# A two-layer transformer tower on one core: the next image's layer norm in nine pieces inside the local attention's loop, its transposes in front of the output product

## The chip, the cores and the metric

The kernel runs on one core of one Trainium2 chip. Its engines are named as in the profile: PE (TensorE, with PEld for its weight loads), DVE (VectorE), ACT (ScalarE), POOL (GpSimd) and SP (SyncE, which issues DMAs here). SBUF is the on-chip memory of 128 partitions, PSUM the eight banks that PE writes into. The metric is the time of one execution on the device in microseconds (us); lower is better. Durations of single instructions are given in us as well, unless marked ns.

## The reference, cut to what matters

Four images are turned into 1024 tokens of 64 numbers each. A first block adds local attention (16 query heads, one shared key and value head, every token looks at itself and the 128 before it) and a mixture of eight experts; a second block adds full attention with a batch norm, and another mixture. The change touches the first norm and the local attention:

```
h = tokens(x)                                  # 4 images x 1024 tokens x 64
n = (h - mean(h)) / sqrt(var(h) + 1e-5)        # layer norm over the 64
q, k, v = n @ wq.T, n @ wk.T, n @ wv.T         # q: 16 heads, k and v: one head
q, k = rmsnorm(rope(q)), rmsnorm(rope(k))
s = where(0 <= row - col <= 128, q @ k.T / 8, -1e30)
h = h + concat_heads(softmax(s) @ v) @ wo.T
h = h + experts(layernorm(h)); ...
```

The norm of an image needs nothing but that image's tokens. All of it is float32.

## The kernel before

The program is a row of stages with a barrier of all engines between them: `setup`, `tokens`, then for each of the four images `project` and `windowed` (a loop of the hardware over `b`), then the later layers. The tokens of an image are made one image ahead: `project` for image b also makes the tokens `h_next` of image b + 1 (a part of the tile `hl`), and `windowed` for image b also norms them and turns them, so that `project` for image b + 1 finds them in `xT`. The work on the next image in the last of the four rounds is done too, and not used.

`windowed` goes over 32 chunks of 32 tokens, as a pipeline that every engine runs in its own program order. In iteration n:

- PE makes the scores of chunk n (`scores`: two mask products L620, four products L624), turns the probabilities of chunk n - 3 (`turn`, ten transposes L637) and makes the values of chunk n - 4 (`values`, L654 and L651). `scores(n)` waits until ACT is done with the exponentials of chunk n - 2, whose two PSUM banks it writes.
- DVE takes the row maxima of chunk n (L684), turns them into the bias of the exponential (L687), copies the turned probabilities of chunk n - 3 from PSUM (L695), and inverts the sums of chunk n - 1 (L701), which waits for ACT's exponentials of that chunk.
- ACT makes the four exponentials of chunk n (L736, each with a read of its accumulated sum), and between them copies an earlier chunk's values to `oT` (`outputs`, L724).
- POOL scales the probabilities of a chunk as soon as DVE has inverted its sums (L715 and L717, both from SBUF to SBUF).

After the loop PE makes the output product of the attention (L669, 16 products of 512 columns) once ACT has copied the last chunk (`oT_ready`), then the four transposes of the normed tokens (`turn_normed`, L273), then the four transposes of the attention's output (`turn_halves`, L396), which wait for ACT's copy of it (L743, `v_act`). DVE norms the next tokens after its last copy of the loop (`layernorm`, L220 to L227, with `one_over_root`, L235 to L240, a Newton iteration on eight columns), copies half of the turned tokens (`turned_vector`, L285; ACT copies the other half, `turned_scalar`, L280) and adds the attention's output to the tokens (L705), which is the stage's last operation.

Every step of `layernorm` but the last goes through `ch.step`: it counts a semaphore up and DVE waits for that count before it goes on. The norm's result goes to `xn` (a part of `vwin`), its scratch is `vrem` and `pTr_own`, which the loop uses as well.

Of the kernel before, what the change touches and what calls it, by code (L numbers as in the profile page):

```python
# [19 lines left out]
I32 = mybir.dt.int32  # L20
U32 = mybir.dt.uint32
ALU = mybir.AluOpType
# [5 lines left out]
D = 64  # L28
# [50 lines left out]
def program(nc, inp, out, sent_rows, answered_rows):  # L79
    with ExitStack() as ctx:  # L80
# [147 lines left out]
                            bc(stat[:, 4, :tiles], D).rearrange("p (w j) d -> p w j d", w=2),  # L228
                            ALU.mult).then_inc(S["xn_ready"], 1)

        def one_over_root(v, ch, dst, x):

            n = x.shape[1]
            half, y, t = (newton[:, k, 0:n] for k in range(3))
            ch.step(v.tensor_scalar(half.bitcast(I32), x.bitcast(I32), 1, None, ALU.logical_shift_right))  # L235
            ch.step(v.tensor_scalar(y.bitcast(I32), half.bitcast(I32), -1.0, float(0x5F3759DF), ALU.mult, ALU.add))
            for k in range(3):
                ch.step(v.tensor_tensor(t, y, y, ALU.mult))
                ch.step(v.scalar_tensor_tensor(out=t, in0=t, scalar=-0.5, in1=x, op0=ALU.mult, op1=ALU.mult))
                ch.step(v.scalar_tensor_tensor(out=dst if k == 2 else y, in0=t, scalar=1.5, in1=y, op0=ALU.add,  # L240
                                               op1=ALU.mult))
# [24 lines left out]
        def both_banks(first):  # L266
            return ps[:, first:first + 2, :].rearrange("p a n -> p (a n)")

        def turn_normed(pe, at):

            pe.wait_ge(S["xn_ready"], 1)
            for j in range(TILES // 2):
                ins = nc.tensor.transpose(bank[at + j // 2][:, P * (j % 2):P * (j % 2) + P], xn[:, j].rearrange("p w d -> p (w d)"), ident[:])  # L273
                if j % 2:
                    ins.then_inc(S["xT_psum"], 1)
# [129 lines left out]
        def tokens(block):  # L405
            @block.tensor
            def _(pe):
                turn_halves(tokensT, 3, S["tok_done"])
                turn_normed(pe, 1)

            @block.scalar
            def _(a):
                a.wait_ge(S["tok_done"], 1)
                keep_tokens(3)
                turned_scalar(a, 1)

            @block.vector
            def _(v):
                ch = Chain(v, S["dve_chain"])
                v.wait_ge(S["h_ready"], 1)  # L420
                layernorm(v, ch, h_next, xn_in_order, tmp, moe, st, TILES)
                turned_vector(v, 1)
# [171 lines left out]
                    g.tensor_tensor(dst, first, second, ALU.add).then_inc(S["rot_done"], 1)  # L594


        def windowed(block, b):

            def s_banks(c):
# [6 lines left out]
            def _(pe):  # L606
# [33 lines left out]
                def values(c):  # L640
                    pe.wait_ge(S["pT_ready"], c + 1)
                    if c >= 1:
                        pe.wait_ge(S["oT_ready"], c)
                    for own_keys in range(2):
                        for hh in range(2):
                            for e in range(2):
                                q = 2 * e + hh
                                o = bank[6 + hh][half_rows(e), 0:P]
                                r = slice(CHUNK * q, CHUNK * q + CHUNK)
                                if own_keys:  # L650
                                    ins = nc.tensor.matmul(o, vrem[r, c, :], pT[r, c % 2, NQ * P:], start=False, stop=True,  # L651
                                                           tile_position=(CHUNK * q, D * e), skip_group_check=True)
                                else:
                                    nc.tensor.matmul(o, vwin[:, c, :], pT[:, c % 2, P * q:P * q + P], start=True,  # L654
                                                     stop=True, skip_group_check=True)
                    ins.then_inc(S["pv_done"], 1)

                for n in range(CHUNKS + 4):
                    if n < CHUNKS:
                        scores(n)  # L660
                    if 3 <= n < CHUNKS + 3:
                        turn(n - 3)
                    if n >= 4:
                        values(n - 4)
                pe.wait_ge(S["oT_ready"], CHUNKS)
                for p in range(PAIRS):
                    for w in range(2):
# [1 line left out]
                        ins = nc.tensor.matmul(bank[0][D * w:D * w + D, :], sbuf["wo0"][:, p, :],  # L669
                                               oT[:, p, w * HALF:(w + 1) * HALF], start=(p == 0), stop=(p == PAIRS - 1))  # L670
                ins.then_inc(S["proj_done"], 1)
                turn_normed(pe, 1)
                pe.wait_ge(S["v_act"], 1)
                turn_halves(outT, 3, S["wo_done"])

            @block.vector
            def _(v):
                ch = Chain(v, S["dve_chain"])

                for n in range(CHUNKS + 3):  # L680
                    c = n
                    if c < CHUNKS:
                        v.wait_ge(S["scores_done"], c + 1)
                        ch.step(v.tensor_reduce(row_max(c),  # L684
                                                ps[:, s_banks(c), 0:2 * SPAN].rearrange("p e (h k) -> p e h k", h=2), X,
                                                ALU.max))
                        v.scalar_tensor_tensor(out=small[:, c % 4, 1, :].rearrange("p (e h) -> p e h", e=2),  # L687
                                               in0=row_max(c), scalar=-1.0, in1=rq[:, c], op0=ALU.mult,
                                               op1=ALU.mult).then_inc(S["bias_ready"], 1)
                    c = n - 3  # L690
                    if c >= 0:
                        v.wait_ge(S["transposed"], c + 1)
                        if c >= 2:
                            v.wait_ge(S["pv_done"], c - 1)
                        v.tensor_copy(pT[:, c % 2, :].rearrange("p (q r t) -> p r q t", r=2, t=D),  # L695
                                      ps[:, 4:6, 0:(NQ + 1) * D].rearrange("p r (q t) -> p r q t", t=D)).then_inc(
                                          S["pT_ready"], 1)
                    c = n - 1
                    if 0 <= c < CHUNKS:
                        v.wait_ge(S["exp_done"], NQ * (c + 1))  # L700
                        v.reciprocal(small[:, c % 4, 3, :], small[:, c % 4, 2, :]).then_inc(S["sums_inverted"], 1)  # L701
                layernorm(v, ch, h_next, xn_in_order, tmp, moe, st, TILES)
                turned_vector(v, 1)
                v.wait_ge(S["wo_done"], 1)
                v.tensor_tensor(res[:, bass.ds(b * TILES, TILES), :].rearrange("p (w j) d -> p j w d", w=2),  # L705
                                h[:].rearrange("p (w j) d -> p j w d", w=2),
                                bank[3][:].rearrange("p (j w d) -> p j w d", w=2, d=D), ALU.add)
# [13 lines left out]
            def _(a):  # L721
# [17 lines left out]
                                             accum_out=small[:, c % 4, 2, q:q + 1]).then_inc(S["exp_done"], 1)  # L739
                for c in range(CHUNKS - 4, CHUNKS):  # L740
                    outputs(c)
                a.wait_ge(S["proj_done"], 1)
                nc.scalar.activation(outT, bank[0][:], ACT.Copy).then_inc(S["v_act"], 1)  # L743
                turned_scalar(a, 1)

        def first_argmax(v, ch, p, top, cand, best, hot, tiles):

# [748 lines left out]
```

## Time and profile before

| | us |
|---|---|
| time, median of 3 runs | 1035.75 (1033.81 to 1037.19) |
| time of the profiled execution | 1028.99 |
| its span, first to last instruction | 1027.2 |
| PE busy | 729.6 |
| DVE busy | 632.3 |
| ACT busy | 444.1 |
| POOL busy | 371.0 |

The granted TensorE clock is 0.85 of full speed in the mean. The span is the time from the first instruction to the last on the core; the time holds about 1.8 us more around it. Busy times are sums over a whole execution and tell nothing of what a single stage waits for. A row of the timeline gives start, duration, engine, line, operation, what it writes and reads with the number of elements per partition, how often, and in brackets the idle time of the engine just before it and what ended it. A row of the windows gives for a stretch its length, the busy time of PE, PEld, DVE, ACT and POOL with the number of instructions, the granted clock, and the DMA's share and rate.

### The profile page before, as it was taken

To read this page: it belongs to the slowest core of one execution; us is meant where nothing else is said; L and a number is where in the kernel's file an instruction comes from. 1 tells how busy PE (TensorE), PEld (TensorE's weight loads), DVE (VectorE), ACT (ScalarE), POOL (GpSimd) and SP (SyncE) were. 2 spreads that over 40 slices of the span, in tenths; PEclk is the share of its full clock that TensorE was granted. 3 is DMA by queue.
4 is the path that set the end of the run, shared out by engine and by line. 5 is a ranking of instruction groups with operands and counts; after the bars stand their busy time and mean duration, and the time that the engine had idled before them with its cause. 6 is when DMAs were issued, how large, how long until landed. Compare 5 with 4: busy or idle time off the path is not lost. (4 is left out here: it accounts for less than half of the span.)

```text
span 1027.2 us, 21128 instructions
## 1 busy us (share of the span) xinstructions
PE 729.6 (71%) x8166; PEld 480.6 (47%) x8166; DVE 632.3 (62%) x1278; ACT 444.1 (43%) x1396; POOL 371.0 (36%) x424
## 2 busy tenths in 40 slices
PE   5477899696999696996879994983899960303900
PEld 5132677243775225773437763662577730303700
DVE  0567588485886566883857875676577738501345
ACT  0012799123995126991229962521566620101100
POOL 0035466053663353661535641462000000073075
PEclk9979699888999798998878997995999986555955
DMA  8051000330000420003300000000000040001122
GB/s 292 34 205 39 2 3 2 144 97 6 3 3 2 174 72 2 3 2 120 114 14 3 2 2 1 1 3 0 1 2 2 2 124 1 1 27 64 46 44 44
DMA packets 51482, 43.66 MB, mean 43 GB/s; under 512 B 46484, under 2 KB 47956, under 8 KB 50452
## 3 DMA queue, kind: packets, MB, share of 16 engines
q1 hardware_dynamic: 49174, 35.83, 11.0%
q10 hardware_dynamic: 144, 4.19, 1.0%
q0 software_dynamic: 2048, 2.10, 0.8%
q8 instruction: 71, 1.16, 0.5%
q14 instruction: 45, 0.37, 0.1%
HBM read 29.33 MB, written 4.72 MB: 33 GB/s over the span
## 5 line engine op out<-in xcount | busy, mean ns | idle before, releaser
L736 ACT ACTIVATE work<-ps,small,rq 128x160 f32<-128x160 f32 x512 | 243.1, 486 | 37.4 <-DVE small L687 37.2
L715 POOL TENSOR_TENSOR work<-work,small 128x512 f32<-128x512 f32 x128 | 133.1, 1040 | 146.6 <-DVE small L701 146.6
L684 DVE TENSOR_REDUCE ps<-ps 128x4 f32<-128x640 f32 x128 | 106.5, 832 | 62.3 <-PE ps L624 62.3
L695 DVE COPY pT<-ps 128x640 f32<-128x640 f32 x128 | 105.4, 823 | 7.9 <-PE ps L637 7.9
L624 PE MATMUL ps<-kT,big 64*128 64x160 f32 x1024 | 108.5, 336 | 0.0
L262 PE MATMUL ps<-xT,s_proj_w 64*128 64x512 f32 x288 | 87.6, 729 | 28.6 <-issue 18.9
L736 ACT ACTIVATION_READ_ACCUMULATOR work<-ps,small,rq 128x1 f32 x512 | 105.0, 205 | 0.0
L594 POOL TENSOR_TENSOR big<-prod 128x1024 f32<-128x1024 f32 x32 | 75.3, 2360 | 63.1 <-DVE prod L566 62.8
L1378 POOL DMA_INDIRECT sent_rows<-big,xb x32 | 30.9, 965 | 184.6 <-DVEq L1330 175.1
L654 PE MATMUL ps<-pT,vwin 128*64 128x128 f32 x1024 | 85.5, 285 | 10.3 <-ACT big L724 2.4
L624 PEld LDWEIGHTS ps<-kT,big 64*128 64x128 f32 x1024 | 85.3, 211 | 0.4
L508 ACT ACTIVATE big<-ps 128x1024 f32<-128x1024 f32 x32 | 32.8, 1024 | 96.8 <-DVE prod L566 96.8
L654 PEld LDWEIGHTS ps<-pT,vwin 128*64 128x64 f32 x1024 | 57.7, 138 | 24.5 <-issue 17.3
L566 DVE TENSOR_TENSOR prod<-ps,s_rope_cos 128x1024 f32<-128x1024 f32 x36 | 43.9, 1218 | 38.5 <-PE ps L262 28.4
L262 PEld LDWEIGHTS ps<-xT,s_proj_w 64*128 64x128 f32 x288 | 30.0, 225 | 76.2 <-issue 46.1
L637 PE MATMUL ps<-s_ident,work 64*128 64x64 f32 x1024 | 56.9, 230 | 2.1 <-DVE pT L695 2.1
L651 PE MATMUL ps<-pT,vrem 32*64 32x128 f32 x1024 | 57.8, 295 | 0.0
L620 PE MATMUL ps<-window_mask,row_of_t 64*128 64x128 bf16 (+1 forms) x256 | 33.4, 256 | 33.5 <-PEq L208 21.9
L724 ACT ACTIVATE big<-ps 128x256 f32<-128x256 f32 x128 | 48.6, 380 | 16.5 <-PE ps L651 16.2
L1092 DVE TENSOR_REDUCE h<-ps 128x1 f32<-128x1024 f32 x32 | 39.1, 1224 | 23.3 <-PE ps L1001 23.3
L637 PEld LDWEIGHTS ps<-s_ident,work 64*128 64x128 f32 x1024 | 49.7, 143 | 6.8 <-POOL pTr_own L717 4.3
L717 POOL TENSOR_TENSOR pTr_own<-work,small 128x128 f32<-128x128 f32 x128 | 51.0, 399 | 0.0
(260 smaller groups left out, 1293.2 us busy)
## 6 DMA issues: line engine op xcount, KB each, us to landing
xb<-in_x SPq DMA_DIRECT2D x4, 4096.0 KB, 13.9
xb<-in_x ACTq DMA_DIRECT2D x1, 4096.0 KB, 15.1
vrem<-hl SPq DMA_DIRECT2D x64, 64.0 KB, 2.0
s_proj_w<-in_proj_w SPq DMA_DIRECT2D x1, 1536.0 KB, 6.4
sent_rows<-zeros SPq DMA_DIRECT2D x8, 160.0 KB, 4.0
big<-sent_rows SPq DMA_DIRECT2D x5, 256.0 KB, 3.4
answered_rows<-big SPq DMA_DIRECT2D x8, 160.0 KB, 1.8
xb<-in_ffn_w SPq DMA_DIRECT2D x1, 1028.0 KB, 5.0
```

The source lines that it names most:

```text
L262: ins = nc.tensor.matmul(bank[banks + w][:], proj_w[half_rows(w), cols], xT[half_rows(w), :], start=True, stop=True)
L594: g.tensor_tensor(dst, first, second, ALU.add).then_inc(S["rot_done"], 1)
L624: ins = nc.tensor.matmul(tiles[e][:, hh, :], qT[half_rows(e), c, 4 * hh:4 * hh + 4, :].rearrange("p a t -> p (a t)"), kT[half_rows(e), CHU ...
L637: ins = nc.tensor.transpose(bank[4 + r][:, D * q:D * q + D], src, ident[half_rows(r), half_rows(r)])
L651: ins = nc.tensor.matmul(o, vrem[r, c, :], pT[r, c % 2, NQ * P:], start=False, stop=True, tile_position=(CHUNK * q, D * e), skip_group_che ...
L654: nc.tensor.matmul(o, vwin[:, c, :], pT[:, c % 2, P * q:P * q + P], start=True, stop=True, skip_group_check=True)
L684: ch.step(v.tensor_reduce(row_max(c), ps[:, s_banks(c), 0:2 * SPAN].rearrange("p e (h k) -> p e h k", h=2), X, ALU.max))
L695: v.tensor_copy(pT[:, c % 2, :].rearrange("p (q r t) -> p r q t", r=2, t=D), ps[:, 4:6, 0:(NQ + 1) * D].rearrange("p r (q t) -> p r q t", ...
L715: g.tensor_tensor(probs[:, c % 3, :, 0:P], probs[:, c % 3, :, 0:P], bc(small[:, c % 4, 3, :], P), ALU.mult)
L717: g.tensor_tensor(own[:, c % 2, :].rearrange("p (q k) -> p q k", q=NQ), probs[:, c % 3, :, P:SPAN], bc(small[:, c % 4, 3, :], CHUNK), ALU. ...
L724: nc.scalar.activation(oT[:, :, CHUNK * c:CHUNK * (c + 1)].rearrange("p (h a) t -> p h a t", h=2), ps[:, 6:8, 0:P].rearrange("p h (a t) -> ...
L736: nc.scalar.activation(probs[:, c % 3, q, :], bank[2 * (c % 2) + e][:, SPAN * hh:SPAN * hh + SPAN], ACT.Exp, bias=small[:, c % 4, 1, q:q + ...
```

## The change

The norm of the next image's tokens leaves the end of `windowed` and is cut into nine parts, `norm_part(v, ch, 0)` to `norm_part(v, ch, 8)`. DVE runs part n - 6 as the last thing of iteration n, so in the iterations 6 to 14 of the loop; in all others nothing is added. The instructions, their shapes and the `ch.step` waits between them are those of before. What they write is moved away from the tiles that the loop uses: differences, squares and result go to other parts of `hl`, the Newton iteration to rows of `st`. PE's four transposes of the normed tokens go in front of the output product, behind a wait for the last exponentials (their two banks held scores) and for `xn_ready`. ACT copies its half of the turned tokens in front of the copy of the attention's output. DVE's copy L285 stays behind the loop.

```diff
+        def norm_part(v, ch, part):
+
+            if part == 0:
+                ch.step(v.tensor_reduce(st[:, 0, :], h_next, X, ALU.add))
+            if part == 1:
+                ch.step(v.tensor_scalar(st[:, 1, :], st[:, 0, :], 1.0 / D, None, ALU.mult))
+                ch.step(v.tensor_tensor(diff, h_next, bc(st[:, 1, :], D), ALU.subtract))
+            if part == 2:
+                ch.step(v.tensor_tensor(squared_diff, diff, diff, ALU.mult))
+            if part == 3:
+                ch.step(v.tensor_reduce(st[:, 2, :], squared_diff, X, ALU.add))
+            if part == 4:
+                ch.step(v.tensor_scalar(st[:, 3, :], st[:, 2, :], 1.0 / D, LN_EPS, ALU.mult, ALU.add))
+                ch.step(v.tensor_scalar(half_guess.bitcast(I32), st[:, 3, :].bitcast(I32), 1, None,
+                                        ALU.logical_shift_right))
+                ch.step(v.tensor_scalar(guess.bitcast(I32), half_guess.bitcast(I32), -1.0, float(0x5F3759DF), ALU.mult,
+                                        ALU.add))
+            if 5 <= part < 8:
+                ch.step(v.tensor_tensor(guess_squared, guess, guess, ALU.mult))
+                ch.step(v.scalar_tensor_tensor(out=guess_squared, in0=guess_squared, scalar=-0.5, in1=st[:, 3, :],
+                                               op0=ALU.mult, op1=ALU.mult))
+                ch.step(v.scalar_tensor_tensor(out=guess, in0=guess_squared, scalar=1.5, in1=guess, op0=ALU.add,
+                                               op1=ALU.mult))
+            if part == 8:
+                v.tensor_tensor(xn_next_in_order, diff.rearrange("p (w j) d -> p w j d", w=2),
+                                bc(guess, D).rearrange("p (w j) d -> p w j d", w=2), ALU.mult).then_inc(S["xn_ready"], 1)
...
@@ PE, behind the loop of windowed @@
+                pe.wait_ge(S["exp_done"], NQ * CHUNKS)
+                turn_normed(pe, 1, xn_next)
                 pe.wait_ge(S["oT_ready"], CHUNKS)
...
                 ins.then_inc(S["proj_done"], 1)
-                turn_normed(pe, 1)
                 pe.wait_ge(S["v_act"], 1)
...
@@ DVE, the loop of windowed @@
                         v.reciprocal(small[:, c % 4, 3, :], small[:, c % 4, 2, :]).then_inc(S["sums_inverted"], 1)
-                layernorm(v, ch, h_next, xn_in_order, tmp, moe, st, TILES)
+                    norm_part(v, ch, n - FIRST_PART)
                 turned_vector(v, 1)
...
@@ ACT, behind the loop of windowed @@
                     outputs(c)
+                turned_scalar(a, 1)
                 a.wait_ge(S["proj_done"], 1)
                 nc.scalar.activation(outT, bank[0][:], ACT.Copy).then_inc(S["v_act"], 1)
-                turned_scalar(a, 1)
```

`FIRST_PART` is 6. The line numbers below are those of each kernel's own source: L684, L687, L695 and L701 of before are L718, L721, L729 and L735 now.

DVE in `windowed`, the iterations 9 to 11 of before:

```order
L684 TENSOR_REDUCE ps<-ps 128x2x2
L687 SCALAR_TENSOR_TENSOR small<-ps,rq 128x4
L695 COPY pT<-ps 128x2x5x64
L701 RECIPROCAL small<-small 128x4
L684 TENSOR_REDUCE ps<-ps 128x2x2
L687 SCALAR_TENSOR_TENSOR small<-ps,rq 128x4
L695 COPY pT<-ps 128x2x5x64
L701 RECIPROCAL small<-small 128x4
```

The same place now, from the end of iteration 10 (part 4) to the end of iteration 11 (part 5):

```order
L735 RECIPROCAL small<-small 128x4
L615 TENSOR_SCALAR st<-st 128x8
L616 TENSOR_SCALAR st<-st 128x8
L618 TENSOR_SCALAR st<-st 128x8
L718 TENSOR_REDUCE ps<-ps 128x2x2
L721 SCALAR_TENSOR_TENSOR small<-ps,rq 128x4
L729 COPY pT<-ps 128x2x5x64
L735 RECIPROCAL small<-small 128x4
L621 TENSOR_TENSOR st<-st 128x8
L622 SCALAR_TENSOR_TENSOR st<-st 128x8
L624 SCALAR_TENSOR_TENSOR st<-st 128x8
```

Three instructions of the norm now stand between the inversion that releases POOL and the row maxima that the next exponentials need.

PE at the end of `windowed` before (L669 is the output product, L273 the transposes of the normed tokens, L396 those of the attention's output):

```order
L654 MATMUL ps<-pT,vwin 64x128 x4
L651 MATMUL ps<-pT,vrem 64x128 x4
L669 MATMUL ps<-big,s_wo 64x512 x16
L273 MATMUL ps<-s_ident,vwin 128x128 x4
L396 MATMUL ps<-s_ident,work 128x128 x4
```

And now (L687, L684 and L704 are the lines that were L654, L651 and L669):

```order
L687 MATMUL ps<-pT,vwin 64x128 x4
L684 MATMUL ps<-pT,vrem 64x128 x4
L273 MATMUL ps<-s_ident,hl 128x128 x4
L704 MATMUL ps<-big,s_wo 64x512 x16
L396 MATMUL ps<-s_ident,work 128x128 x4
```

The four transposes of the normed tokens moved from behind the output product to the place in front of it.

## Rows read from the trace of the kernel before

**Rows 1.** Windows of the first image's loop: steady state, and its cold beginning.

```profile
140.00:160.00 20.00, 19.42 (x336) 15.20 (x334) 16.43 (x37) 20.00 (x84) 12.80 (x19) 1.00 0.01 3
...
112.00:116.00 4.00, 3.26 (x38) 2.59 (x34) 3.04 (x7) 3.24 (x14) 1.88 (x4) 0.50 0.01 2
```

**Rows 2.** Timeline of DVE, first image: chunk 6, then chunks 14 and 15.

```profile
120.72 0.83 DVE L684 TENSOR_REDUCE ps<-ps 128x4 f32<-128x640 f32 x1 [0.76 <-PE ps L624]
...
138.20 0.83 DVE L684 TENSOR_REDUCE ps<-ps 128x4 f32<-128x640 f32 x1 [0.37 <-PE ps L624]
139.07 0.16 DVE L687 SCALAR_TENSOR_TENSOR small<-ps,rq 128x4 f32<-128x4 f32 x1
139.15 0.82 DVE L695 COPY pT<-ps 128x640 f32<-128x640 f32 x1
139.89 0.17 DVE L701 RECIPROCAL small<-small 128x4 f32<-128x4 f32 x1
140.35 0.83 DVE L684 TENSOR_REDUCE ps<-ps 128x4 f32<-128x640 f32 x1 [0.29 <-PE ps L624]
141.22 0.16 DVE L687 SCALAR_TENSOR_TENSOR small<-ps,rq 128x4 f32<-128x4 f32 x1
```

**Rows 3.** Timeline of ACT, the last exponential of chunk 14, the first of 15.

```profile
141.30 0.22 ACT L736 ACTIVATION_READ_ACCUMULATOR work<-ps,small,rq 128x1 f32 x1
141.41 0.48 ACT L736 ACTIVATE work<-ps,small,rq 128x160 f32<-128x160 f32 x1
```

**Rows 4.** Timeline of POOL beside them.

```profile
140.13 1.04 POOL L715 TENSOR_TENSOR work<-work,small 128x512 f32<-128x512 f32 x1 [0.83 <-DVE small L701]
141.13 0.40 POOL L717 TENSOR_TENSOR pTr_own<-work,small 128x128 f32<-128x128 f32 x1
```

**Rows 5.** Timeline of DVE at the end of the first image's `windowed`.

```profile
181.75 0.68 DVE L220 TENSOR_REDUCE st<-hl 128x8 f32<-128x512 f32 x1
182.46 0.17 DVE L221 TENSOR_SCALAR st<-st 128x8 f32<-128x8 f32 x1
182.66 0.69 DVE L222 TENSOR_TENSOR vrem<-hl,st 128x512 f32<-128x512 f32 x1
183.39 0.69 DVE L223 TENSOR_TENSOR vrem<-vrem 128x512 f32<-128x512 f32 x1
...
187.25 0.69 DVE L227 TENSOR_TENSOR vwin<-vrem,st 128x512 f32<-128x512 f32 x1
```

**Rows 6.** Timeline of PE and ACT at the same end.

```profile
183.32 0.45 PE L651 MATMUL ps<-pT,vrem 32*64 32x128 f32 x8
184.27 7.09 PE L669 MATMUL ps<-big,s_wo 128*64 128x512 f32 x32 [0.50 <-ACT big L724]
191.29 0.66 PE L273 MATMUL ps<-s_ident,vwin 128*128 128x128 f32 x4
192.05 0.66 PE L396 MATMUL ps<-s_ident,work 128*128 128x128 f32 x4
...
191.40 0.60 ACT L743 ACTIVATE work<-ps 128x512 f32<-128x512 f32 x1 [7.19 <-PE ps L669]
```

**Rows 7.** Timeline in `project`: a DVE operation on eight columns, POOL's beside it.

```profile
62.59 1.63 DVE L235 TENSOR_SCALAR pTr_own<-rk 128x8 int32<-128x8 int32 x1
...
61.85 2.35 POOL L594 TENSOR_TENSOR big<-prod 128x1024 f32<-128x1024 f32 x1
```

**Rows 8.** Experts: DVE and POOL operations side by side; their durations (min/median/max).

```profile
666.75 0.56 DVE L920 TENSOR_TENSOR res<-res,xb 128x256 f32<-128x256 f32 x1
667.34 0.83 DVE L923 TENSOR_TENSOR res<-res,xb 128x256 f32<-128x256 f32 x1
...
666.32 0.71 POOL L953 TENSOR_TENSOR xb<-xb 128x128 f32<-128x128 f32 x1
666.99 0.90 POOL L949 TENSOR_TENSOR xb<-xb 128x256 f32<-128x256 f32 x1
...
L923 DVE TENSOR_TENSOR res<-res,xb x16: 424/424/834, 667.3 to 701.1; 128x256 f32<-128x256 f32 x16
```

More of the change, by code:

```diff
@@ L229, in layernorm, with one_over_root @@
                             ALU.mult).then_inc(S["xn_ready"], 1)
-        def one_over_root(v, ch, dst, x):
+        def one_over_root(v, ch, dst, x, scratch=None):
             n = x.shape[1]
-            half, y, t = (newton[:, k, 0:n] for k in range(3))
+            half, y, t = scratch or (newton[:, k, 0:n] for k in range(3))
             ch.step(v.tensor_scalar(half.bitcast(I32), x.bitcast(I32), 1, None, ALU.logical_shift_right))
@@ L267, in both_banks, with turn_normed @@
             return ps[:, first:first + 2, :].rearrange("p a n -> p (a n)")
-        def turn_normed(pe, at):
+        def turn_normed(pe, at, xn):
             pe.wait_ge(S["xn_ready"], 1)
@@ L408, in _ @@
                 turn_halves(tokensT, 3, S["tok_done"])
-                turn_normed(pe, 1)
+                turn_normed(pe, 1, xn)
             @block.scalar
@@ L594, in _ @@
                     g.tensor_tensor(dst, first, second, ALU.add).then_inc(S["rot_done"], 1)
+        FIRST_PART = 6
+        diff, squared_diff = (hl[:, TILES * k:TILES * (k + 1), :] for k in (0, 1))
+        xn_next = hl[:, 2 * TILES:3 * TILES, :].rearrange("p (j w) d -> p j w d", w=2)
+        xn_next_in_order = hl[:, 2 * TILES:3 * TILES, :].rearrange("p (j w) d -> p w j d", w=2)
+        guess, half_guess, guess_squared = st[:, 5, :], st[:, 6, :], st[:, 7, :]
+        def norm_part(v, ch, part):
[23 more added lines that the diff above has]
+                                bc(guess, D).rearrange("p (w j) d -> p w j d", w=2), ALU.mult).then_inc(S["xn_ready"], 1)
         def windowed(block, b):
@@ L671, in _ @@
                 ins.then_inc(S["proj_done"], 1)
-                turn_normed(pe, 1)
                 pe.wait_ge(S["v_act"], 1)
```

## The prediction, made before the changed kernel ran

> **What bounds the kernel now.** The change sits in one stage that runs four times, so the shares of the whole page decide nothing. I read the windows of the local attention's loop first, then the timeline of DVE, ACT and POOL over one iteration, then the end of the stage, and last every place where DVE and POOL work on SBUF at once.
>
> In the steady loop ACT is busy for all of 20 us and PE for 19.42 of them, at the full clock of 2.4 GHz; DVE has 16.43 [rows 1]. So an iteration takes as long as ACT's four exponentials and PE's products, and DVE looks as if it had a fifth of its time to give. But it stands in the ring that sets the pace: the row maxima and the bias of a chunk come from DVE, and the exponentials of that chunk wait for them. The bias of chunk 15 ends at 141.22 + 0.16 = 141.38, ACT's last read of chunk 14 starts at 141.30 and its first exponential of chunk 15 at 141.41, 0.11 us behind that read and 0.03 behind the bias [rows 2, 3]. So the bias comes just in time, never early. A DVE that comes later delays the exponentials at once, and as ACT has no idle time in which to catch up, a delay stays.
>
> What does DVE have to spare in an iteration? From the row maxima to the inversion it goes in one piece: 138.20 to 139.89, 1.69 us; an operation that waits for nothing starts 0.08 us behind the start of such a short one (139.07 to 139.15), so 1.77 us is the least that an iteration can take on DVE [rows 2]. The nine iterations from chunk 6 to chunk 15 take 140.35 - 120.72 = 19.63 us, 2.18 each [rows 2]. Spare: 0.41 us per iteration, 3.7 us in nine.
>
> At the end of the stage the chain is: the last copy to oT, the output product 184.27 to 191.36, ACT's copy 191.40 to 192.00, the transposes of the attention's output at 192.05 [rows 6]. The norm ends at 187.25 + 0.69 = 187.94, 3.4 us before the output product does [rows 5, 6], and the four transposes of the normed tokens lie at 191.29 to 191.95, beside ACT's copy [rows 6].
>
> **What the change takes away: nothing that anything waits for.** The norm at the end of the stage (6.2 us of DVE, 181.75 to 187.94) lies beside the output product [rows 5, 6]. The four transposes lie beside ACT's copy; if they go, the next transposes start when ACT is done, at 192.00 instead of 192.05. Gain: 0 to 0.05 us per image. ACT's and DVE's copies of the turned tokens ended before the last transposes did and had slack too.
>
> **What it adds at the end.** Four transposes, 0.66 us from first start to last end, now stand in front of the output product. PE is idle there for 0.50 us, waiting for ACT's last copy [rows 6]; their waits (the last exponentials, the norm, done in iteration 14 of 32) are over long before, so nothing queued behind them is held. 0.66 - 0.50 = 0.16 us per image; 0 if weight loads overlap better, 0.66 if nothing does. I take 0.15.
>
> **What it adds in the loop, first by DVE time alone.** Steps behind a wait go from start to start in: 0.71 for the sum of 512 columns (181.75 to 182.46), 0.20 for eight columns (182.46 to 182.66), 0.73 for the wide subtraction (182.66 to 183.39) [rows 5]. The last, wide step has no wait behind it and costs some 0.61, as 0.08 of an operation's end overlaps the next in the loop (0.82 against 139.15 to 139.89) [rows 2, 5]. Part 0: 0.71. Part 1: 0.20 + 0.73 = 0.93. Part 2: 0.73. Part 3: 0.72. Part 4: 3 x 0.20 = 0.60. Parts 5 to 7: 0.60 each. Part 8: 0.61. Sum 6.10 us. None of the parts fits: each is longer than the 0.41 spare. So DVE becomes the bound in all nine iterations: 9 x 1.77 + 6.10 = 22.03 us instead of 19.63, **+2.40 us per image**.
>
> **Then by what POOL does meanwhile.** A part begins 0.08 us behind the inversion. The same inversion releases POOL, whose scaling starts 0.24 us behind it (139.89 to 140.13) and holds 1.04 and then 0.40 us with hardly a gap [rows 4]. Both read and write SBUF. Two places show what that means. In `project` an operation on eight columns, 0.17 elsewhere, takes 1.63 us: it ends at 64.22, POOL's began before it and ends at 64.20 [rows 7]. So it got to run 0.15 us before POOL's end. That is a tensor-scalar. In the experts DVE adds two SBUF operands: 0.83 us instead of the median of 424 ns beside POOL's operation, and 0.56 for the one before; POOL's operations between them are drawn out as well, 0.71 and 0.90 [rows 8]. They take turns: POOL, DVE, POOL, DVE, each behind the other.
>
> In the loop: the first step of a part (0.08 to 0.25 behind the inversion) is through when POOL starts. The second wants to start at 0.28, POOL has had SBUF since 0.25; it gets it about 0.14 before POOL's first scaling ends at 0.25 + 1.04, so at 1.15, and is done at 1.32. The third wants 1.36, but POOL's second scaling (0.40) took its turn at 1.32 and lets go at 1.58; the third is done at 1.75, the row maxima can start at 1.79. Without POOL they could at 0.08 + 0.60 = 0.68. So parts 4 to 7, three short steps each, cost 1.11 us more each: 4.44. Part 1: its wide subtraction starts at 1.15 instead of 0.28: 0.87 more. Parts 0 and 3 are reductions with a single SBUF input; no row shows such a one delayed (the inversion has a single one, too). Parts 2 and 8 are a single step that is ahead of POOL; POOL is delayed by up to 0.5 us, which its 0.83 idle [rows 4] takes. Together **+5.31 us per image**.
>
> The Trainium skill's page "SBUF — State Buffer", section "Who interferes with whom", states this as a rule: a VectorE operation in a two-port mode, or with two SBUF inputs while GpSimd's reads SBUF, and the GpSimd operation block each other for the whole instruction, whoever issued second waits. With it the sum is the one above; a reader who goes by instruction durations alone gets 2.40 per image in its place. The trace agrees with the rule, but for the last 0.15 us of an instruction, in [rows 7, 8]; that the rule holds for two-input operations of eight columns no row shows.
>
> **The sum.** 2.40 + 5.31 + 0.15 = 7.86 us per image, times 4 = 31.4 us. Against the profiled execution: 1028.99 + 31.4 = 1060.4. That execution was 6.8 us quicker than the median of the runs, so for the median 1035.75 + 31.4 = **1067**. The bounds of the waiting: if the second step gets in ahead of POOL (it is 0.03 us behind), part 1 waits for nothing and parts 4 to 7 for POOL's first scaling only, some 0.9 each: 2.4 + 3.6 + 0.15 = 6.2 per image, 1060. If a step waits for both scalings in one go (to 0.25 + 1.44): 1.4 for each of five parts, 2.4 + 7.0 + 0.15 = 9.5 per image, 1074.
>
> **The rivals.**
>
> *Waiting that isn't there.* Two-input operations of eight columns may slip past POOL. For it: no row shows them together. Against it: the wide ones wait [rows 8]. Then only DVE's time counts, and part 4, whose tensor-scalars do wait [rows 7]: between 4 x 2.55 = 10 and 4 x 3.7 = 15 us, 1046 to 1051. Chance 0.17.
>
> *The clock falls as well.* In the drawn-out iterations of 3.5 us PE has 2.1 us of work (19.42 of 20, in iterations of 2.18 [rows 1]), 60% instead of 97. The loop's beginning shows 1.2 GHz granted with PE busy for 3.26 of 4 us [rows 1], which at full clock would be about 40%. [...] If it falls, an iteration of PE takes up to 4.2 us until the clock is back: 0.7 more in four iterations and up to 2 in one or two behind them, 3 to 7 us per image: 12 to 28 us on top, 1079 to 1095. Chance 0.12.
>
> *Faster.* The one mechanism: the transposes of the attention's output start when PE has done the normed tokens' transposes, not when ACT has copied, and the end of the stage gains up to their 0.66 + 0.1 us. Price 4 x 0.76 = 3.0 us, 1033 or a little less. It decides only if the loop takes the parts for nothing, that is if DVE has more than 0.7 us to spare where the rows give 0.41 per iteration, and 141.38 to 141.41 leaves none [rows 2, 3]. Chance 0.04.
>
> *No difference.* The bias is in time after all, because the ring has slack that the rows don't show, and the parts are hidden: 1036. Chance 0.06.
>
> **How the numbers follow.** A measurement of this kernel can tell about 0.3%, 3.1 us, from no change. The forecast, between 1058 and 1076, has 0.61. The range of 8 in 10: from 1045, which takes in the rival without waiting, to 1082, which takes in the upper bound of the waiting and the mild end of a falling clock. Left out are faster and no difference (0.10), the rest of the clock (0.07) and some for what I have not thought of. Faster by over 0.3%: 0.04, within it 0.06, slower 0.90.
>
> **What the profile after would show.** In the iterations 6 to 14 of each image the row maxima (now L718) start 2.4 to 2.5 us apart for the parts 0, 2, 3 and 8, and some 3.5 us apart for the parts 1 and 4 to 7; idle time of DVE before them is gone there, and 2.18 us is back behind chunk 15. The second and third step of parts 4 to 7 are recorded with about 1.0 and 0.4 us instead of 0.17. From chunk 6 to chunk 15: about 27.3 us, not 19.63. ACT waits for the bias (L721). At the end of the stage the output product starts within 0.2 us of where it did behind the last values, ends 7.09 us later, and nothing is earlier. Wrong would be: the short steps at 0.17 us (then the first rival), or 1.2 GHz in the iterations 10 to 16 (then the second).

## The result, and the profile after

The changed kernel takes 1064.03 us in the median of 4 runs (1058.87 to 1069.55), the kernel before 1035.78 (1033.81 to 1037.19). The ratio is 1.0275, with a 95% interval of 1.022 to 1.033: 28 us slower. The profiled execution took 1058.87 us with a span of 1057.1, 29.9 more than the span before.

Parts 1 and 5 of the page of the changed kernel:

```profile
PE 740.2 (70%) x8166; PEld 484.8 (46%) x8166; DVE 646.4 (61%) x1278; ACT 446.9 (42%) x1396; POOL 375.9 (36%) x424
...
L770 ACT ACTIVATE work<-ps,small,rq 128x160 f32<-128x160 f32 x512 | 243.5, 487 | 63.2 <-DVE small L721 62.3
L749 POOL TENSOR_TENSOR work<-work,small 128x512 f32<-128x512 f32 x128 | 135.9, 1062 | 169.8 <-DVE small L735 169.8
```

DVE executes as many instructions as before, 1278, but is busy for 646.4 us instead of 632.3. ACT's exponentials, whose idle time in front of them was 37.4 us in all, now have 63.2, and nearly all of it ends with DVE's bias (L721). The page alone says that DVE holds up ACT, and that its instructions have become longer. The timelines say which. DVE in the first image's loop, part 1 (L608, L609) and part 4 (L615 to L618), between the inversion (L735) and the next row maxima (L718):

```profile
125.06 0.17 DVE L735 RECIPROCAL small<-small 128x4 f32<-128x4 f32 x1
125.14 0.14 DVE L608 TENSOR_SCALAR st<-st 128x8 f32<-128x8 f32 x1
125.32 1.57 DVE L609 TENSOR_TENSOR hl<-hl,st 128x512 f32<-128x512 f32 x1
...
133.54 0.17 DVE L735 RECIPROCAL small<-small 128x4 f32<-128x4 f32 x1
133.62 0.14 DVE L615 TENSOR_SCALAR st<-st 128x8 f32<-128x8 f32 x1
133.80 1.05 DVE L616 TENSOR_SCALAR st<-st 128x8 int32<-128x8 int32 x1
134.89 0.32 DVE L618 TENSOR_SCALAR st<-st 128x8 int32<-128x8 int32 x1
135.25 0.83 DVE L718 TENSOR_REDUCE ps<-ps 128x4 f32<-128x640 f32 x1
```

POOL and ACT beside them:

```profile
125.30 1.04 POOL L749 TENSOR_TENSOR work<-work,small 128x512 f32<-128x512 f32 x1 [1.07 <-DVE small L735]
126.30 0.85 POOL L751 TENSOR_TENSOR pTr_own<-work,small 128x128 f32<-128x128 f32 x1
133.79 1.04 POOL L749 TENSOR_TENSOR work<-work,small 128x512 f32<-128x512 f32 x1 [1.06 <-DVE small L735]
134.78 0.40 POOL L751 TENSOR_TENSOR pTr_own<-work,small 128x128 f32<-128x128 f32 x1
...
136.31 0.48 ACT L770 ACTIVATE work<-ps,small,rq 128x160 f32<-128x160 f32 x1 [1.14 <-DVE small L721]
```

Read them as one sequence. The inversion at 133.54 releases POOL, which starts at 133.79. The first step of part 4 went in front of it and is through at 133.76. The second, on eight columns, starts 0.01 us behind POOL and ends at 134.85; POOL's scaling ends at 134.83. The third ends at 135.21, POOL's second scaling at 135.18. Only then come the row maxima, 1.71 us behind the inversion instead of 0.46 [rows 2], and ACT has stood idle for 1.14 us. In part 1 the wide subtraction takes 1.57 us instead of 0.69 [rows 5], and draws out POOL's second scaling from 0.40 to 0.85 in its turn. The Newton steps do the same as part 4, in all four images (min/median/max in ns):

```profile
L622 DVE SCALAR_TENSOR_TENSOR st<-st x12: 1053/1053/1055, 137.2 to 593.9; 128x8 f32<-128x8 f32 x12
...
L624 DVE SCALAR_TENSOR_TENSOR st<-st x12: 322/324/324, 138.3 to 595.0; 128x8 f32<-128x8 f32 x12
```

These read two operands in SBUF, and wait just as the tensor-scalars L616 and L618 do, which read one. The window of the changed kernel over the parts 4 to 8 (length, busy PE, PEld, DVE, ACT, POOL, clock) shows the bound: DVE 15.32 of 15.91 us, ACT 11.14, PE 11.52, where ACT had all of the time before [rows 1]. The granted clock is 1.00, the level of 2.4 GHz, with PE busy for 72% of the window:

```profile
131.85:147.76 15.91, 11.52 (x180) 8.29 (x180) 15.32 (x34) 11.14 (x46) 6.88 (x11) 1.00 0.00 2
```

At the end of the stage, PE, ACT and DVE of the changed kernel (L704 is the output product, L778 ACT's copy, L739 the addition):

```profile
190.73 0.45 PE L684 MATMUL ps<-pT,vrem 32*64 32x128 f32 x8
191.11 0.66 PE L273 MATMUL ps<-s_ident,hl 128*128 128x128 f32 x4
191.69 7.09 PE L704 MATMUL ps<-big,s_wo 128*64 128x512 f32 x32
199.48 0.66 PE L396 MATMUL ps<-s_ident,work 128*128 128x128 f32 x4 [0.70 <-ACT work L778]
...
198.83 0.60 ACT L778 ACTIVATE work<-ps 128x512 f32<-128x512 f32 x1 [6.86 <-PE ps L704]
...
200.29 0.69 DVE L739 TENSOR_TENSOR res<-h,ps 128x512 f32 x1 [8.06 <-PE ps L396]
```

The output product starts 0.96 us behind the last values' start; before it was 0.95 [rows 6]. The four transposes fit into the wait. But the addition now starts 0.81 us behind the transposes L396. Before it was 1.18:

```profile
193.23 0.69 DVE L705 TENSOR_TENSOR res<-h,ps 128x512 f32 x1 [0.83 <-PE ps L396]
...
202.87 1.22 DVE L566 TENSOR_TENSOR prod<-ps,s_rope_cos 128x1024 f32<-128x1024 f32 x1 [8.95 <-issue]
```

(The second row, DVE's first multiplication of `project`, is used below.)

Where the 29.9 us of the span are, worked out from the starts of the row maxima, the addition and the next row maxima in both timelines, sums over the images: from chunk 6 to chunk 15 +28.7 (26.86 instead of 19.63 in three images, 26.86 instead of 19.82 in the fourth); from chunk 15 to 31 nothing (34.97 both); from chunk 0 to chunk 6 -1.0; from chunk 31 to the addition -1.35 (17.56 instead of 17.90 each); from the addition to the next image's first row maxima +1.35; ahead of the first row maxima +1.6; later stages +0.6.

### The profile page after: what moved, and what is told of

The parts are those of the page before. It is cut to its first block and busy times, and to the rows that moved or that the text cites. A ratio compares the mean times of both kernels' runs of the same rounds, so it can differ in the third digit from the quotient of the medians.

```text
span 1057.1 us, 21164 instructions
## 1 busy us (share of the span) xinstructions
PE 740.2 (70%) x8166; PEld 484.8 (46%) x8166; DVE 646.4 (61%) x1278; ACT 446.9 (42%) x1396; POOL 375.9 (36%) x424
## 5 line engine op out<-in xcount | busy, mean ns | idle before, releaser
L770 ACT ACTIVATE work<-ps,small,rq 128x160 f32<-128x160 f32 x512 | 243.5, 487 | 63.2 <-DVE small L721 62.3
L749 POOL TENSOR_TENSOR work<-work,small 128x512 f32<-128x512 f32 x128 | 135.9, 1062 | 169.8 <-DVE small L735 169.8
L718 DVE TENSOR_REDUCE ps<-ps 128x4 f32<-128x640 f32 x128 | 106.6, 832 | 50.5 <-PE ps L657 49.4
L729 DVE COPY pT<-ps 128x640 f32<-128x640 f32 x128 | 105.5, 824 | 7.9 <-PE ps L670 7.9
L687 PE MATMUL ps<-pT,vwin 128*64 128x128 f32 x1024 | 85.6, 285 | 11.0 <-ACT big L758 2.4
L687 PEld LDWEIGHTS ps<-pT,vwin 128*64 128x64 f32 x1024 | 57.7, 138 | 25.2 <-issue 18.7
L684 PE MATMUL ps<-pT,vrem 32*64 32x128 f32 x1024 | 57.5, 294 | 0.0
```

The lines of the kernel that those rows point to most:

```text
L718: ch.step(v.tensor_reduce(row_max(c), ps[:, s_banks(c), 0:2 * SPAN].rearrange("p e (h k) -> p e h k", h=2), X, ALU.max))
L749: g.tensor_tensor(probs[:, c % 3, :, 0:P], probs[:, c % 3, :, 0:P], bc(small[:, c % 4, 3, :], P), ALU.mult)
L770: nc.scalar.activation(probs[:, c % 3, q, :], bank[2 * (c % 2) + e][:, SPAN * hh:SPAN * hh + SPAN], ACT.Exp, bias=small[:, c % 4, 1, q:q + ...
```

## The experiments

All ratios are to the kernel before on the same chip; its median was 1035.99 beside the first four experiments and 1036.74 beside the last four. The stretches in this table come from the timelines of the profiled executions, in us per image: from the row maxima of chunk 6 to those of chunk 15, from those of chunk 31 to the addition, and from the addition to DVE's first multiplication in `project` (three images).

| kernel | time, ratio (95%) | chunk 6 to 15 | chunk 31 to addition | to first multiplication |
|---|---|---|---|---|
| before | 1035.78 | 19.63 to 19.82 | 17.90 | 9.6, 9.8, 9.8 |
| changed | 1064.03, 1.0275 (1.022 to 1.033) | 26.86 | 17.56 | 9.9, 9.8, 10.2 |
| parts in front of the inversion | 1044.4, 1.0078 (1.0048 to 1.0108) | 21.82 | 17.56 | 10.8, 11.6, 11.9 |
| single-input steps | 1045.87, 1.0112 (1.0078 to 1.0147) | 22.63 | 17.56 | 10.0, 11.6, 11.3 |
| old order at the end | 1063.61, 1.0278 (1.0239 to 1.0317) | 26.84 | 17.55 | 10.9, 11.1, 9.8 |
| before, no norm there | 1031.05, 0.9958 (0.9936 to 0.998) | 19.83 | 17.56 | 7.7, 8.0, 7.5 |
| before, load later | 1032.63, 0.9968 (0.9946 to 0.999) | 19.62 to 19.82 | 17.91 | 7.7, 8.0, 7.9 |
| norm where DVE idles | 1036.85, 1.0015 (0.9989 to 1.0041) | 19.71 to 19.84 | 17.57 | 9.7, 10.7, 9.9 |
| and end in halves | 1035.72, 0.9985 (0.9969 to 1.0002) | 19.72 to 19.84 | 16.16 | 12.0, 10.7, 10.7 |
| and load later | 1030.35, 0.9942 (0.992 to 0.9964) | 19.71 to 19.83 | 16.16 | 8.8, 8.1, 7.5 |

### The part in front of the inversion

```diff
+                    norm_part(v, ch, n - FIRST_PART)
                     c = n - 1
                     if 0 <= c < CHUNKS:
                         v.wait_ge(S["exp_done"], NQ * (c + 1))
                         v.reciprocal(small[:, c % 4, 3, :], small[:, c % 4, 2, :]).then_inc(S["sums_inverted"], 1)
-                    norm_part(v, ch, n - FIRST_PART)
```

> The changed kernel with each part of the norm one instruction earlier on DVE: behind the copy of the turned probabilities and in front of the inversion that releases POOL, instead of behind it. The same instructions, the same DVE time; but POOL is then done with its scaling (it ends about 1.65 us behind the last inversion, the part begins about 1.77 us behind it). My theory (DVE time of 2.4 us per image, plus 5 us of waiting for POOL): the second and third short steps fall from 1.05 and 0.32 us to about 0.15, the wide subtraction from 1.57 to 0.66, the stretch from chunk 6 to chunk 15 from 26.9 to about 22 us in each image, the time from 1064 to about 1044 to 1047. Rival one, it is DVE time alone and the long records are only how a wait for the chain's semaphore is drawn: the time stays at 1064. Rival two, POOL is now released later and that costs as much: 1055 to 1064, with PE waiting for POOL's scaling in the loop.

Measured 1044.4 us, ratio 1.0078 (1.0048 to 1.0108). DVE and POOL of this kernel around part 4:

```profile
133.74 0.16 DVE L615 TENSOR_SCALAR st<-st 128x8 f32<-128x8 f32 x1
133.93 0.17 DVE L616 TENSOR_SCALAR st<-st 128x8 int32<-128x8 int32 x1
134.13 0.17 DVE L618 TENSOR_SCALAR st<-st 128x8 int32<-128x8 int32 x1
134.34 0.18 DVE L736 RECIPROCAL small<-small 128x4 f32<-128x4 f32 x1
...
134.60 1.04 POOL L749 TENSOR_TENSOR work<-work,small 128x512 f32<-128x512 f32 x1 [0.96 <-DVE small L736]
```

The same instructions take 0.16 to 0.17 us once POOL stands still. Chunk 6 to 15 falls by 5.04 us per image, 20.2 in four; the median falls by 19.6. POOL released later costs nothing. So of the 7.2 us per image 5.0 are waiting beside POOL and 2.2 are DVE's own time. Both rivals fall.

### Steps with a single input

```diff
@@ part 4 @@
-                ch.step(v.tensor_scalar(half_guess.bitcast(I32), st[:, 3, :].bitcast(I32), 1, None,
-                                        ALU.logical_shift_right))
-                ch.step(v.tensor_scalar(guess.bitcast(I32), half_guess.bitcast(I32), -1.0, float(0x5F3759DF), ...))
+                ch.step(v.tensor_reduce(half_guess, st[:, 3, :].unsqueeze(2), X, ALU.add))
+                ch.step(v.tensor_reduce(guess, half_guess.unsqueeze(2), X, ALU.add))
@@ parts 5 to 7: the second and the third step in the same way, the first takes a maximum in place of a product @@
```

> The changed kernel with the parts in their place, but the second and third step of the parts 4 to 7 replaced by sums over one element, which read a single operand in SBUF and have eight columns like those they replace. The Newton iteration is left out by this, so the norm's result is not the reference's; number, place, size and waits of the DVE instructions are those of the changed kernel. My theory (an operation with two SBUF inputs or a tensor-scalar waits for POOL, one with a single input does not): these eight steps per image take about 0.15 us each, an iteration with them 2.4 us instead of 3.39, four per image: 1064 - 16 = 1048. The wide subtraction of part 1 keeps its 1.57 us. Rival, three instructions with semaphores behind the inversion cost this time whatever they read: 1064.

Measured 1045.87 us, ratio 1.0112 (1.0078 to 1.0147). The sums in the Newton steps' place, and the wide subtraction that was left as it is (ns):

```profile
L620 DVE TENSOR_REDUCE st<-st x12: 161/161/161, 134.9 to 579.7; 128x8 f32<-128x8 f32 x12
...
L609 DVE TENSOR_TENSOR hl<-hl,st x4: 1573/1574/1575, 124.1 to 564.2; 128x512 f32<-128x512 f32 x4
```

POOL runs beside both as in the changed kernel. A sum that reads one operand in SBUF takes 0.16 us in the place where the two-operand steps took 1.05 and 0.32; the subtraction, which reads two, waits as before. So the kind of operation decides, not its place or the semaphores around it. The number of operands alone doesn't: the tensor-scalars L616 and L618 of the changed kernel read one and waited. Of the 5.04 us, 4.23 are the eight short steps (26.86 - 22.63), the rest the subtraction.

### The old order at the end of the stage

```diff
-                pe.wait_ge(S["exp_done"], NQ * CHUNKS)
-                turn_normed(pe, 1, xn_next)
                 pe.wait_ge(S["oT_ready"], CHUNKS)
...
                 ins.then_inc(S["proj_done"], 1)
+                turn_normed(pe, 1, xn_next)
                 pe.wait_ge(S["v_act"], 1)
```

with ACT's `turned_scalar` behind its copy of the output again.

> The changed kernel with the end of the stage as before: the transposes of the normed tokens behind the output product, ACT's copy of its half of the turned tokens behind that of the attention's output. The parts stay in the loop. In the trace of the changed kernel the last addition starts 0.81 us behind the first transpose of the attention's output, before it was 1.18. Theory: before, DVE's own copy of the turned tokens (L285) ended only just ahead of the addition and held it up by 0.37 us; the old order brings 1.18 back, and the time is 1.0 to 1.5 us longer than the changed kernel's, 1065.5. Rival: the 0.37 us is a chance of the one execution or comes from the norm's place; then 0.81 stays and the time is that of the changed kernel. The difference is smaller than one comparison can tell in the time, so the trace decides.

Measured 1063.61 us, ratio 1.0278 (1.0239 to 1.0317), no different from the changed kernel. PE and DVE of this kernel:

```profile
198.61 0.66 PE L273 MATMUL ps<-s_ident,hl 128*128 128x128 f32 x4
199.37 0.66 PE L396 MATMUL ps<-s_ident,work 128*128 128x128 f32 x4
...
199.30 0.42 DVE L285 COPY xT<-ps 128x256 f32<-128x256 f32 x1 [10.15 <-PE ps L273]
200.19 0.69 DVE L738 TENSOR_TENSOR res<-h,ps 128x512 f32 x1 [0.46 <-PE ps L396]
```

My theory falls: DVE's copy is as late as it was before, and the addition still starts 0.82 us behind L396, in all four images 17.55 or 17.56 us behind chunk 31. So the order at the end is worth nothing, either way, and the 0.34 us per image go with the norm's place.

### No norm at the end

```diff
-                layernorm(v, ch, h_next, xn_in_order, tmp, moe, st, TILES)
+                v.tensor_copy(xn_in_order[:, 0, 0, :], h_next[:, 0, :]).then_inc(S["xn_ready"], 1)
```

> The kernel before with the norm of the next image left out of the local attention's stage: one copy of 64 columns stands for it, so the later images' attention works on wrong data. The transposes and copies of the turned tokens stay where they were. It asks what the change could have gained at most by taking the norm away from the end of the stage. My theory: nothing waits for it, the output product still ends the stage: 1035.8, within 1 us. Rival: the norm at the end does hold something (the transposes, the barrier, DVE's program), then it is 1 us or more per image shorter, 1032 or less.

Measured 1031.05 us, ratio 0.9958 (0.9936 to 0.998): the time is 4.9 us shorter, so the rival is right in that the norm at the end does hold something. The table has two places. The end of the stage gains 0.34 us per image, 1.4 in all, as in every kernel without the norm there. And three times DVE's first multiplication in `project` comes 7.5 to 8.0 us behind the addition, not 9.6 to 9.8. The next experiment takes that up. The traces don't follow these 2 us any further: from the addition to the next image's first row maxima this kernel takes 56.7 to 56.9 us, the kernel before 55.8 to 57.5. So the most that taking the norm away could bring was 1.4 us at the end of the stage, plus whatever the shorter program does at the next one's start; the changed kernel has the former and none of the latter.

### The next image's load behind DVE's first multiplication

In the trace of before DVE's first multiplication starts at 202.87, its idle time ends with "issue", 3.75 us behind PE's first product, though later ones follow in about 1.1 us steps. The stage's 4 MB load began at 195.57.

```diff
@@ project, SP; on the kernel before @@
+                sp.wait_ge(S["prod_done"], 1)
                 load_x(sp, b + 1, S["back0"])
```

> The kernel before with one edit in the stage that makes queries and keys: the 4 MB load of the image after next is issued when DVE has finished its first multiplication there, not at the stage's start. In the traces so far DVE's first multiplication of that stage starts 9.6 to 9.8 us behind the end-of-stage addition with the kernel before, 9.8 to 11.9 in the kernels with the norm in the loop, 7.5 to 8.0 with the norm left out, with PE's first products there in time in all of them. Theory: DVE's next instructions come in by DMA and lie behind the load, which fills the DMA engines (share 0.93); then this kernel has 7.5 us or a little less, three times 2 us less, 1030. Rival: the time goes for the branch and the barrier and has nothing to do with the load; then it stays at 9.7 and the time at 1036, or longer, if the load now comes late for the products that read it.

Measured 1032.63 us, ratio 0.9968 (0.9946 to 0.999). DVE and SP of this kernel:

```profile
192.00 0.69 DVE L706 TENSOR_TENSOR res<-h,ps 128x512 f32 x1 [0.83 <-PE ps L396]
199.68 1.22 DVE L567 TENSOR_TENSOR prod<-ps,s_rope_cos 128x1024 f32<-128x1024 f32 x1 [7.00 <-PE ps L262]
...
201.10 0.34 SPq L384 DMA_DIRECT2D xb<-in_x  x1
```

7.68, 8.01 and 7.87 us instead of 9.64 to 9.81, so the load at the stage's start does hold DVE back here. It isn't the load alone: the kernel without the norm issues it at the stage's start too, and has 7.5 to 8.0.

The theory was that what waits are DVE's instructions, which come by DMA as well. The DMA view of the traces has a queue of the kind "instruction" (q14) with a few packets per stage. In the kernel before, two of them stand in the midst of the load, 7.5 to 9.0 us behind the addition in the three images, with the first multiplication at 9.6 to 9.8. With the load later they stand at 4.75 to 5.75 us, and the kernel without the norm has none between 4 us and 7.5. That fits the theory; but the view doesn't name the engine that a packet is for, so it isn't shown.

In the time 4.1 us are left of the 6, and where they are no trace shows: from the addition to the next image's first row maxima this kernel takes 56.7 to 57.1 us, the kernel before 55.8 to 57.5. The profiled execution of before was 6.8 us quicker than the median, so it is no fair measure of such long stretches.

### The norm where DVE idles, the end in halves, and both with the later load

```diff
@@ DVE, windowed: 4 steps of the norm in front of the loop, 15 in it @@
+                early, later = norm_steps(v)
+                for step in early:
+                    ch.step(step())
                 for n in range(CHUNKS + 3):
...
+                    if 0 <= n - 1 < len(later):
+                        if n == len(later):
+                            later[n - 1]().then_inc(S["xn_ready"], 1)
+                        else:
+                            ch.step(later[n - 1]())
                     c = n - 1
```

> The changed kernel with the same work of the norm cut so that it fits DVE's idle time: the first four steps (2.4 us) in front of the loop, where DVE idles for 2.8 us at each image, then one step per iteration from iteration 1 to 15, in front of the inversion, 0.2 us each, the wide product in two halves. My theory of the ring (0.41 us to spare per iteration, nothing waits for POOL in front of the inversion): from chunk 6 to chunk 15 19.6 to 19.8 us as in the kernel before, instead of 26.9; at the end of the stage the 0.34 us that all kernels without the norm there have gained stay, so the time is that of the kernel before less 1.4 us, 1034.5. Rival: a step on DVE costs its full time in every iteration, because the ring has nothing to spare: 15 steps of 0.2 and more, 1036 + 4 x 3.5 = 1050.

Measured 1036.85 us, ratio 1.0015 (0.9989 to 1.0041). The steps in front of the loop (first and last), and the first row maxima behind them:

```profile
103.06 0.69 DVE L608 TENSOR_REDUCE st<-hl 128x8 f32<-128x512 f32 x1 [1.27 <-PEq L208]
...
104.71 0.69 DVE L611 TENSOR_TENSOR hl<-hl 128x512 f32<-128x512 f32 x1
105.44 0.83 DVE L720 TENSOR_REDUCE ps<-ps 128x4 f32<-128x640 f32 x1
```

Chunk 6 to 15 takes 19.71 to 19.84 us, within 0.1 us of before, and the end 17.57: here the norm is next to free in the loop, in steps of at most 0.41 us (half of the wide product) that keep clear of POOL. The forecast for the time, 1034.5, was missed by 2.4 us, and against the kernel before on the same chip there is no gain at all: the stretch from the addition to the next image's first row maxima is 57.1 to 58.3 us, where it was 55.8 to 57.5.

```diff
@@ PE, windowed, on the kernel above: half 0 goes to bank 0, half 1 to bank 4 @@
+                    if n == CHUNKS:
+                        pe.wait_ge(S["exp_done"], NQ * (CHUNKS - 1))
+                        out_products(0, 0, 2)
...
+                    if n == CHUNKS + 3:
+                        pe.wait_ge(S["exp_done"], NQ * CHUNKS)
+                        turn_normed(pe, 1, xn_next)
...
+                out_products(0, 2, 2 * PAIRS).then_inc(S["proj_done"], 1)
+                pe.wait_ge(S["oT_ready"], CHUNKS)
+                out_products(1, 0, 2 * PAIRS).then_inc(S["proj_done"], 1)
```

> The kernel with the norm where DVE idles, and a new end of the stage: the output product in two halves of 256 columns, in two banks. The first half needs no late chunk and fills PE's waits of 0.5 us ahead of the last transposes and behind the last values; the transposes of the normed tokens fill the 0.59 us ahead of the last values; ACT copies and PE turns the first half beside the second's products. Theory, what an early norm is good for is filling the waits of the last four iterations: some 1.4 us per image from the last row maxima to the addition (17.56 to about 16.2), in all 5.6 us less than the kernel with the undivided end, 1029. Rival: 32 products of 256 columns instead of 16 of 512 take longer by their weight loads, and eat the gain: 17.5.

Measured 1035.72 us, ratio 0.9985 (0.9969 to 1.0002). PE and DVE at the end of its stage (L695 is the output product, L719 the transposes):

```profile
182.91 0.66 PE L273 MATMUL ps<-s_ident,hl 128*128 128x128 f32 x4
...
184.54 6.70 PE L695 MATMUL ps<-big,s_wo 128*64 128x256 f32 x60
191.17 0.99 PE L719 MATMUL ps<-s_ident,work 128*128 128x128 f32 x4
...
192.32 0.69 DVE L758 TENSOR_TENSOR res<-h,ps 128x512 f32 x1 [8.29 <-PE ps L719]
```

PE has no wait left between the last transposes and the end of the output product, and the end of the stage takes 16.16 us, 1.4 less per image, as expected. The rival falls: the narrower products do not take longer as a whole (6.70 us for 60 of their 64 passes, where all 32 of before take 7.09). The time has next to none of it, 1.1 us of the 5.6, which the runs can't tell from none: the first multiplication comes 10.7 to 12.0 us behind the addition.

> The kernel with the end in column halves and the later load together. If both theories hold the gains add: 1036 - 1.4 - 5.6 - 6 = 1023. If the load theory falls it is the time of the kernel with the column halves, 1029, or longer.

Measured 1030.35 us, ratio 0.9942 (0.992 to 0.9964). The first multiplication is back at 7.5 to 8.8 us. That is 6 us faster than the kernel before and the fastest of those that compute everything, though not the 1023 of the sum: it is 5.4 us less than with the halves alone, but only 2.3 less than with the later load alone, where the sum has 7.0.

## Why the prediction was right, point by point

The predicted time was 1067 for the changed kernel, 1064.03 was measured; by the differences 31.4 and 28.2 us. The two large terms were right in cause and near in size. All three terms of the sum were somewhat too large, by some 4 us in four images. By the spans, stretches outside the sum gave 2.5 of these back, which is luck.

- **The ring.** Right. DVE had its 0.41 us per iteration and no more: with the parts clear of POOL the nine iterations take 21.82 us, 2.19 more, where the sum said 2.40. Each of these iterations is 0.02 to 0.04 us shorter than reckoned, but for the first, as the row maxima behind a part are recorded with 0.80 us instead of 0.83: the term was 0.2 too large.
- **The waiting beside POOL.** Right in mechanism, order and place. Expected were 5.31 us per image, measured 5.04. The second steps were expected to end 1.32 us behind the inversion and do at 1.31 (134.85 - 133.54); the third at 1.75, and do at 1.67, as POOL's second scaling starts before its first ends (134.78 against 134.83). An iteration with three short steps takes 3.38 to 3.40 us, not 3.5. What no row of before could show, that a two-input operation of eight columns waits as a wide one does, holds: 1053 ns.
- **The bound on the race for SBUF.** POOL came first all 20 times, by 0.01 to 0.02 us (133.79 against 133.80). With so small a lead the order was not safe to forecast from durations read to 0.01 us; that the middle value held, and not the 1060 of the other order, was in part luck.
- **The end of the stage.** Wrong, by little. "What the change takes away: nothing that anything waits for" should have been a gain of 0.34 us per image, and the transposes, costed at 0.15, cost 0.01. Instead of +0.6 us in all it is -1.35. No view of before shows this: the addition's wait is booked on L396, as it is after. The old order at the end doesn't bring it back and leaving out the norm does, so it hangs on the norm's instructions ahead of DVE's last two; by which mechanism stays open.
- **The rivals.** Without waiting, 1046 to 1051: its condition was false. The two kernels in which the short steps don't wait take 1044.4 and 1045.87, just below its price. The upper end of that price left out the wide subtraction of part 1, which waits by the prediction's own reading of [rows 8]: 0.87 us per image, 3.5 us more. The clock stayed at 2.4 GHz over the drawn-out iterations, where PE was busy for 69% (6.96 us of the 10.16 from 135.25 to 145.41) and not for the 60% that the rival reckoned with. The mechanism named for a faster kernel, the transposes L396 waiting for the normed tokens' transposes, is refuted by the old order at the end.
- **Outside the sum.** Together +2.5 us of the spans: +1.35 between the stages and +1.6 ahead of the first, -1.0 ahead of chunk 6 and +0.6 in later stages. They are of the size by which these stretches vary from one profiled execution to the next (the first row maxima start at 105.23 to 106.82 in all kernels here).

## What to carry to other kernels

Before work is moved into a loop, look for the ring that sets its pace: an engine that is busy for 82% may have only 0.41 us of an iteration to give, and a delay in the ring is not caught up. Then ask of what kind each moved instruction is, what it reads, and who is released just ahead of it: eight steps of 0.17 us cost 1.0 and 0.3 us each beside POOL's scaling, and nothing of the sort one instruction earlier. And first of all ask what waits for the work where it stands now: here moving it could gain 1.4 us in four images, so there was little to win and 28 us to lose.

## What the runs showed of the hardware that I had not expected

- DVE's and POOL's queued instructions take turns on SBUF one by one, and an eight-column operation ends 0.01 to 0.03 us behind the end of POOL's, whether that was of 1.04 us or of 0.40; it holds for tensor-scalars and for operations with two SBUF inputs alike, not for a sum with one. The Trainium skill, page "SBUF — State Buffer", section "Who interferes with whom", has the rule that the later one blocks for the whole instruction; the trace agrees but for the last 0.15 us (an operation of 0.17 us ends 0.02 behind).
- In the kernel before, the 4 MB load issued at a stage's start delays DVE's first instruction there by some 2 us (9.6 to 9.8 against 7.7 to 8.0), but not in the kernel without the norm, with the load in the same place (7.5 to 8.0). This first instruction moves by up to 2 us more between kernels whose stages around it differ (up to 12.0). The gain of 1.4 us per image at the end of one stage went under until the load was moved; then 2.3 of its 5.6 us showed.
- The addition at the end starts 0.34 to 0.37 us earlier when the norm's instructions don't stand shortly ahead of it, though DVE had waited for 4 us in between. This is open.
